# A fused attention, scan and spiking feed-forward kernel: rotary features by even and odd chunks, the bfloat16 split partly on GpSimd, and the norm of a tile moved up, in the projection stage

## The reference, cut to what matters

```python
ct_q = x @ Wd_q_w + Wd_q_b                       # x is normalised; 256 -> 128
query = heads(ct_q @ Wu_q_w + Wu_q_b) + heads(_rope(ct_q @ Wq_r_w + Wq_r_b, cos, sin))
ct_kv = x @ Wd_kv_w + Wd_kv_b
key = heads(ct_kv @ Wu_k_w + Wu_k_b) + heads(_rope(x @ Wk_r_w + Wk_r_b, cos, sin))
value = heads(ct_kv @ Wu_v_w + Wu_v_b)
# _rope: x0, x1 are the even and the odd features
out = jnp.stack([x0 * cos - x1 * sin, x1 * cos + x0 * sin], axis=-1)
```

## Time and profile before

| | us |
|---|---|
| three executions, median | 2242.89 |
| the profiled execution | 2247.14 |
| its span, first to last instruction | 2245.2 |
| mean granted TensorE clock | 0.944 |

### The profile page before, as it was taken

One profiled execution on the slowest core, in us unless ns is written; L12 is line 12 of the kernel. 1 busy time (PEld: TensorE's weight loads), 2 busy tenths in 40 slices (PEclk: granted clock), 3 DMA queues, 4 the chain that ended last, 5 costly groups with the idle time before them and its releaser, 6 DMA issues. The chain is left out here.

```text
span 2245.2 us, 26133 instructions
## 1 busy us (share of the span) xinstructions
PE 2016.3 (90%) x6926; PEld 747.5 (33%) x6926; DVE 1722.3 (77%) x2519; ACT 1117.6 (50%) x1448; POOL 673.0 (30%) x443
## 2 busy tenths in 40 slices
PE   6889799999999999999999988878878887679997
PEld 3444122233232332322444433333323332234443
DVE  4778889899898998974555556988898898935554
ACT  3444056666566666674233346566557556312221
POOL 0000200000000000000000017998898898910000
PEclk8999699999999999999999989999999998889998
DMA  3224322342222332204100013444444444310000
GB/s 106 78 81 102 58 34 44 51 55 44 40 44 39 55 51 40 44 16 132 52 0 0 0 40 94 112 108 107 109 106 110 112 108 109 96 39 10 19 19 28
DMA packets 99846, 139.76 MB, mean 62 GB/s; under 512 B 13408, under 2 KB 53104, under 8 KB 99728
## 3 DMA queue, kind: packets, MB, share of 16 engines
q1 hardware_dynamic: 99728, 138.30, 27.4%
HBM read 111.78 MB, written 26.08 MB: 61 GB/s over the span
## 5 line engine op out<-in xcount | busy, mean ns | idle before, releaser
L816 DVE TENSOR_REDUCE mx<-max_bank 128x1 f32<-128x512 f32 x960 | 618.3, 687 | 62.6 <-PE max_bank L714 62.2
L804 ACT ACTIVATE probs<-score_bank 128x1024 f32<-128x1024 f32 x512 | 496.9, 1021 | 298.0 <-PE score_bank L728 296.9
L1573 PE MATMUL ys_bank<-outs,rec_diag 128*128 128x512 f32 x512 | 281.3, 677 | 118.5 <-POOL outs L1509 106.6
L714 PE MATMUL max_bank<-ks,qs 96*128 96x512 bf16 x960 | 335.4, 390 | 0.0
L728 PE MATMUL score_bank<-qs,ks 99*128 99x512 bf16 x1024 | 313.5, 388 | 13.0 <-issue 11.8
L1501 POOL TENSOR_TENSOR ring<-u,bc 128x1024 f32<-128x1024 f32 x128 | 301.0, 2359 | 14.3 <-ACT u L1695 14.3
L1509 POOL TENSOR_TENSOR outs<-ring,bc 128x1024 f32<-128x1024 f32 x112 | 263.7, 2356 | 56.8 <-DVE ring L1908 56.8
L771 PE MATMUL o_bank<-probs,vg 128*32 128x512 f32 x2048 | 275.4, 610 | 0.5 <-ACT probs L804 0.5
L1746 ACT ACTIVATE a_bank<-dt,decay_s 128x512 f32<-128x512 f32 x256 | 171.2, 685 | 167.9 <-DVE ring L1908 153.5
L1249 PE MATMUL hid_bank_f<-xn_f,wfc_f 128*128 (+1 forms) x512 | 239.1, 600 | 8.3 <-DVE xn_f L997 5.1
L1327 DVE SCALAR_TENSOR_TENSOR hid_f<-hid_bank_f,relu_f 128x512 f32<-128x512 f32 x128 | 87.0, 690 | 199.0 <-ACT relu_f L1299 197.9
(11 more groups left out here) (200 smaller groups left out, 2145.2 us busy)
## 6 DMA issues: line engine op xcount, KB each, us to landing
bc<-bc_scr SPq DMA_DIRECT2D x128, 512.0 KB, 4.8
qk_parts<-parts SPq DMA_DIRECT2D x32, 384.0 KB, 2.9
ks<-qk_parts SPq DMA_DIRECT2D x96, 128.0 KB, 4.9
qs<-qk_parts SPq DMA_DIRECT2D x192, 64.0 KB, 5.1
o_scr<-o_sb SPq DMA_DIRECT2D x32, 256.0 KB, 2.0
xin<-in_x_dram SPq DMA_DIRECT2D x8, 512.0 KB, 4.2
o_in<-o_scr SPq DMA_DIRECT2D x16, 256.0 KB
out_dram<-x_out_f SPq DMA_DIRECT2D x8, 512.0 KB, 2.9
```

Of the source, the lines that this page charges most:

```text
L714: nc.tensor.matmul(max_bank[(r + a) % MB][:], qs[r][0:SROWS, half, j, qt * P:(qt + 1) * P], ks[r][0:SROWS, j, kh * TW:(kh + 1) * TW], star ...
L804: nc.scalar.activation(probs[:, s % 2, 2 * pair:2 * pair + 2], score_bank[pair][:], ACT.Exp, scale=SOFTMAX_SCALE).then_inc(probs_ready, 1)
L816: nc.vector.tensor_reduce(mx[:, a // HU, a % HU:a % HU + 1], max_bank[(r + a) % MB][:], AX_X, ALU.max)\
L1573: mm = nc.tensor.matmul(y_bank[f][:], rec_diag[:, f * NS + n], outs[:, g % OUTS, f], start=(n == 0), stop=(n == NS - 1))
```

## The change

Features of queries and keys are reordered: the weights' columns, biases and tables are laid out on the host so that chunk 0 holds the even feature of every pair and chunk 1 the odd one. A rotation then needs each rotary product once, and the swapped weights are not there any more. The scratch tensor in memory gets a layout with the partition rows of a stack in order, so a stack loads in 13 DMAs, and each of the four parts of a tile is written by four DMAs of 96 KB. The rests, the low parts and the scaling of x run on GpSimd. The sum with the compact product is written back into its bank. Banks: two for rotary products, two for compact ones, one for both latents, one for mean and variance, and the two for the transposes also hold the values. Transposes and mean run two tiles ahead, the variance one tile ahead. The table set with logarithm and exponential is requested once at the start. Loops over batches are written out.

```diff
-                 (wq[:, 0, :], io["Wu_q"]), (wq[:, 1, :], io["Wq_r"]), (wq[:, 2, :], io["Wq_r_swap"]),
-                 (wkr[:, 1], io["Wk_r_swap"].rearrange("(c p) n -> p c n", p=P)),
+        KV, ROT_K, Q, V, COMP_K, ROT_Q, COMP_Q = 0, 1, 3, 4, 6, 8, 10
+        UNITS = 12
...
         @block.sync
+            for t in range(NT):
+                if t + 3 < NT:
+                    load_x(t + 3)
+                if t == NT - TPB:
+                    for u in range(CHUNKS):
+                        sp.wait_ge(parts_out[u], OUT * t)
+                    load_stack(sp, split_scr, q_stack, k_stack, 0, stack_in)
                 for u in range(CHUNKS):
+                    sp.wait_ge(low_kept, t * CHUNKS + u + 1)
+                    side, c = 1 - u // DC, u % DC
+                    for n in range(NG):
+                        sp.dma_start(split_scr[(side * B + b) * NG + n, :, c * (HD // 2):(c + 1) * (HD // 2), :,
+                                               half * TW:(half + 1) * TW].rearrange("s i j t -> (i j) s t"),
+                                     parts[n * (P // NG):(n + 1) * (P // NG), u]).then_inc(parts_out[u], 16)
...
         @block.gpsimd
+            def lower_parts(t, side):
+                for u in (parts_of(side), parts_of(side) + 1):
+                    k = t * CHUNKS + u
+                    pool.wait_ge(high_kept, k + 1)
+                    if t:
+                        pool.wait_ge(low_kept, k - CHUNKS + 1)
+                    nc.gpsimd.tensor_tensor(rest[:, u], full[:, u], parts[:, u, 0], ALU.subtract).then_inc(rest_ready, 1)
+                for u in (parts_of(side), parts_of(side) + 1):
+                    pool.wait_ge(mid_kept, t * CHUNKS + u + 1)
+                    nc.gpsimd.tensor_tensor(parts[:, u, 2], rest[:, u], parts[:, u, 1], ALU.subtract).then_inc(low_kept, 1)
+            def scale(t):
+                pool.wait_ge(rs_step, t * 3 + 3)
+                if t > 1:
+                    pool.wait_ge(proj_ready, (t - 2) * UNITS + Q + 1)
+                for c in range(DC):
+                    nc.gpsimd.tensor_tensor(xn[:, t % 2, c], xc[:, c], rs[:], ALU.mult).then_inc(normed, 1)
+            scale(0)
+            for t in range(NT):
+                if t:
+                    lower_parts(t - 1, 0)
+                if t + 1 < NT:
+                    scale(t + 1)
+                lower_parts(t, 1)
+            lower_parts(NT - 1, 0)
...
         @block.tensor
+            def latent(t, u):
+                if u == 0:
+                    pe.wait_ge(latent_kept, t * 2 + 1)
+                elif t:
+                    pe.wait_ge(latent_kept, t * 2)
...
+            turn(0)
+            mean(0)
+            turn(1)
+            var(0)
+            mean(1)
+            pe.wait_ge(consts_in, CONSTS)
+            for t in range(NT):
                 pe.wait_ge(normed, t * DC + DC)
+                latent(t, 1)
+                rotary(t, 1)
+                latent(t, 0)
+                values(t)
+                compact(t, 1)
+                if t + 1 < NT:
+                    var(t + 1)
+                rotary(t, 0)
+                if t + 2 < NT:
+                    turn(t + 2)
+                compact(t, 0)
+                if t + 2 < NT:
+                    mean(t + 2)
...
         @block.scalar
+            nc.scalar.preload_act_table_set("natural_log_exp_and_others")
...
+            for t in range(NT):
+                if t:
+                    high(t - 1, 0)
+                keep_latent(t, 1)
+                keep_latent(t, 0)
+                if t + 1 < NT:
+                    square(t + 1)
+                if t:
+                    middle(t - 1, 0)
+                if t + 1 < NT:
+                    guess(t + 1)
+                if t + 2 < NT:
+                    keep_x(t + 2)
                 high(t, 1)
                 middle(t, 1)
+            high(NT - 1, 0)
+            middle(NT - 1, 0)
...
         @block.vector
+            def rotate(t, side):
+                for c, tables in enumerate(((cos, sin), (sin, cos))):
+                    dve.wait_ge(proj_ready, t * UNITS + (ROT_K if side == 1 else ROT_Q) + c + 1)
+                    for i, table in enumerate(tables):
+                        nc.vector.scalar_tensor_tensor(r[:, 2 * c + i], rot_bank[c][:], bias[:, c:c + 1], table,
+                                                       ALU.add, ALU.mult).then_inc(rotated, 1)
+            def join(t, side):
+                for c in range(DC):
+                    nc.vector.scalar_tensor_tensor(comp_bank[c][:], comp_bank[c][:], bias[:, c:c + 1], r[:, 3 * c],
+                                                   ALU.add, ALU.add).then_inc(rotated, 1)
+                for c in range(DC):
+                    nc.vector.tensor_tensor(full[:, u], comp_bank[c][:], r[:, 2 - c], ALU.subtract if c == 0 else ALU.add)\
+                        .then_inc(summed, 1)
...
+            for t in range(NT):
+                rotate(t, 1)
+                if t + 1 < NT:
+                    centre(t + 1)
+                keep_v(t)
+                join(t, 1)
+                if t + 1 < NT:
+                    finish(t + 1)
+                rotate(t, 0)
+                join(t, 0)
...
 def load_stack(eng, split_scr, q, k, g, done):
+    for row, part, n in K_RUNS:
+        eng.dma_start(k[row * HD:(row + n) * HD], k_in[part * HD:(part + n) * HD]).then_inc(done, 16)
+    for row, part, n in Q_RUNS:
         for h in range(2):
...
 def lay_out(v):
+    even = np.arange(D).reshape(NG, G, HD // 2, 2)[..., 0].transpose(0, 2, 1).reshape(P)
+    rows = np.concatenate([even, even + 1])
+        "cos": cos.T[even // 2], "sin": sin.T[even // 2],
...
-    qk_parts = nc.dram_tensor("qk_parts", (B * 2 * DC, P, 3, S), BF16, kind="Internal").ap()
+    qk_parts = nc.dram_tensor("qk_parts", (2 * B * NG, 3, HD, G, S), BF16, kind="Internal").ap()
```

More of the change, by code:

```diff
@@ L38, with runs_of @@
 MROWS = SROWS + 3
-STACK_LOAD = 16 * 3 * len(Q_PARTS)
+CHUNKS = 2 * DC
+def runs_of(parts):
+    found = []
+    for row, part in enumerate(parts):
+        if found and found[-1][1] + found[-1][2] == part:
+            found[-1][2] += 1
+        else:
+            found.append([row, part, 1])
+    return found
+Q_RUNS, K_RUNS = runs_of(Q_PARTS), runs_of(K_PARTS)
+STACK_LOAD = 16 * (len(K_RUNS) + 2 * len(Q_RUNS))
 LIF_STEPS, BETA, THRESHOLD = 5, 0.9, 1.0
@@ L104, in project @@
 def project(nc, io, xT, vT, split_scr, q_stack, k_stack):
-    CHUNKS = 2 * DC
+    SIDES = 2
     with ExitStack() as ctx:
@@ new lines, in compact, with values @@
+            def compact(t, side):
+                for c in range(DC):
+                    cols = slice(c * P, (c + 1) * P)
+                    if side == 0 or t:
+                        pe.wait_ge(summed, t * CHUNKS + (1 - side) * DC - DC + c + 1)
+                    mm = nc.tensor.matmul(comp_bank[c][:], wkc[:, cols] if side == 1 else wq[:, 0, cols], ct[:, side],
+                                          start=True, stop=True)
+                    mm.then_inc(proj_ready, 1)
+            def values(t):
+                pe.wait_ge(latent_kept, t * 2 + 1)
+                for pair in range(2):
+                    if t + 1 < NT:
+                        pe.wait_ge(x_kept, (t + 1) * DC + pair + 1)
+                    else:
+                        pe.wait_ge(v_kept, (t - 1) * 2 + pair + 1)
@@ new lines, in keep_latent, with high @@
+            def keep_latent(t, u):
+                act.wait_ge(proj_ready, t * UNITS + (Q if u == 0 else KV) + 1)
+                nc.scalar.activation(ct[:, u], lat_bank[:], ACT.Identity, bias=bcol[:, u:u + 1])\
+                    .then_inc(latent_kept, 1)
+            def high(t, side):
+                for u in (parts_of(side), parts_of(side) + 1):
+                    act.wait_ge(summed, t * CHUNKS + u + 1)
+                    act.wait_ge(parts_out[u], OUT * t)
+                    nc.scalar.activation(parts[:, u, 0], full[:, u], ACT.Copy).then_inc(high_kept, 1)
@@ L472, in _ @@
-            centre(0, 0)
-            finish(0, 0)
-            dve.wait_ge(consts_in, CONSTS)
-            tiles(dve, tile)
+            def rotate(t, side):
+                half = t % TPB
+                bias = bcol[:, 2 + 4 * side:4 + 4 * side]
+                cos, sin = (table[:, half * TW:(half + 1) * TW] for table in (cosT, sinT))
+                r = rot[:, 1 - side]
+                if t:
+                    dve.wait_ge(summed, (t - 1) * CHUNKS + parts_of(side) + DC)
+                for c, tables in enumerate(((cos, sin), (sin, cos))):
[3 more added lines that the diff above has]
+                                                       ALU.add, ALU.mult).then_inc(rotated, 1)
@@ L487, in load_stack @@
+    for row, part, n in Q_RUNS:
         for h in range(2):
-            eng.dma_start(q[rows, h], q_in[:, :, Q_PARTS[n], h * TW:(h + 1) * TW]).then_inc(done, 16)
+            eng.dma_start(q[row * HD:(row + n) * HD, h], q_in[part * HD:(part + n) * HD, :, h * TW:(h + 1) * TW])\
```

(1 more changed line is left out.)

353 lines of the change are left out of this document (119 added, 234 removed).

## The result

The changed kernel took 2172.0 us (median of 4 executions, 2169.9 to 2176.3) against 2245.4 us for the kernel before (4 executions, 2236.7 to 2249.3): 0.968 [0.965, 0.972]. It is faster, as forecast, but by more: 2185 us was the number and 2174 the lower end. Executed again with the later experiments it took 2173.1 us (6 executions, up to 2186.1) against 2242.4 (17 executions): 0.970 [0.967, 0.972].

What follows compares the result with a forecast made beforehand. Projection was taken as bound by TensorE's work plus waits from VectorE's queue. Stage: 22.2 + (18.8 + 2.6) + 6 x 18.8 + 30.3 = 186.7 us against 244.3, 57.6 less, so 2185 us; range 2174 to 2206.

Steps and rivals of the forecast that it cites:

- the norm chain: Projection, variance to scaled x: 6.5 us after the variance at 12.3, so 18.8 us against TensorE's own 18.4.
- Attention itself keeps its order: Attention stage: bounded by TensorE with its order kept, so no gain was counted.
- Start: Start of projection: first product moves from 23.0 to 22.2 us.
- The first tile's low clock: First projection tile: products at 1.2 GHz after TensorE waited, loss left at 2.6 us, bounds 0 and 2.6.
- A tile: Projection stage: 18.8 us a tile, against 27.35 before.
- The tail: Last tile's start to attention's first DMA: 30.3 us, where before it was 28.8, so 1.5 us longer.
- an attention of another length: Attention stage in the changed profile: a length other than before would show the prediction wrong; no size given.
- Both table loads in the norm chain: Rival, projection: two loads stay behind the variance, 2.57 us a tile, 18 in all, 2203 us; chance 0.04.
- The thinnest cover, 0.2 us before latent q: Projection tile: ScalarE's latent copy ends at 5.0 us, TensorE wants it at 5.2, 0.2 us of slack.
- Writing the join back into its bank: Projection, VectorE: writing the sum into its bank takes the same price, above by perhaps 0.1 us each.
- SyncE as the bound: Rival, projection: 16 small writes back up at 2.08 us an issue, 33.3 us a tile, 2299 us; chance 0.02.
- ScalarE's order binds: Rival, projection: slower GpSimd or hand-over delays latent q and variance, 20 to 21.5 us a tile, 2194 to 2204; chance 0.25.

Runs made afterwards that it cites:

- The tail experiment: Changed kernel with the last tile's four subtractions for q on VectorE and its last part written by four DMAs of ScalarE's queue: 2167.9 us.
- all on VectorE: Changed kernel with the eight subtractions and two scalings of a tile moved back from GpSimd to VectorE: 2190.6 us.
- the scaling on VectorE: Changed kernel with only the two scalings of x moved back from GpSimd to VectorE: 2184.1 us.
- the join from SBUF: Changed kernel with the sum of compact product and rotation written to SBUF, not back into its bank: 2175.4 us.

## Why the prediction came out as it did

The mechanism of a tile was right: TensorE's own work sets it, the norm chain adds a few tenths, GpSimd and SyncE hide. Two things put the number 13 us too high. Terms of the stage were sized too large, together 8.5 us; these alone would have left 2176.5 us, inside the range. The step that failed is the other one, "Attention itself keeps its order and is bounded by TensorE, so I give it nothing": with the same work the profiled executions show attention 4.8 us and the scan 6.1 us shorter.

The forecast stage was 186.7 us, the measured one 178.2 (179.8 when executed again). By its terms:

- **Start**, 22.2 forecast, 21.45 measured: 0.75 us.
- **The first tile's low clock**, 2.6 us added, none there in the profiled execution. The prediction named the bounds 0 and 2.6 and took the upper, from a start in which TensorE had stood still 6 us. After, it stands still only 2.41 and 1.88 us in this stretch, and ran at 2.4 GHz from 13.2 us on. In five of the six executions with this stage code the term was 0, in the sixth 2.1 us. The first tile took 18.46 us against 21.4, 2.9 us less with the tile's own difference.
- **A tile**, 18.8 forecast, 18.49 on the mean of six (39.91 to 150.87): 1.8 us. TensorE's part was exact: the variance product ends 12.30 us after the tile's start. From there to the next start it took 6.20 us, not 6.5: logarithm and exponential 1.35, Newton 2.15, scalings 2.50, and hand-overs 0.20 for which I had allowed 0.45.
- **The tail**, 30.3 forecast, 27.3 measured: 3.0 us. VectorE's last sum ended 17.7 us after the tile's start, not 18.5; from there the last lower part took 4.6 us, not 5.3, since subtractions with a bfloat16 operand or result take GpSimd 1.155 us, not 1.27, and ScalarE's copies overlap them; the last issue then started 2.2 us later, at 24.5 us, not 2.5, with an issue at 0.44 us, not 0.54; and from the last issue to attention's first it took 2.8 us, not 4.0. In the execution again the tail was 29.0 us, for the low clock of its last tile, which the prediction had not foreseen either.

These make 8.5 us. What lies outside the stage is 10.9 us by the two profiles; the profiled execution before was 4.2 us above the median that the forecast used, the one after 2.0 us below its own, so by the medians 4.5 us are left of the 13. Between the measured medians it is 3 to 9 us (73.4 and 69.3 us less in all, less 66.1 or 64.5). In attention it is the time that TensorE's clock stays at the lower level behind its short waits, 21.5 us against 35.4; in the scan it is whether the clock is low over its first 8 us. What places an execution in one or the other wasn't found: not the number of loads, and a start delayed by 2 to 7 us moved attention by under 2 us and the scan not at all. The tail experiment had a scan of 635.5 and the best median, so one profiled execution doesn't even tell what a kernel does as a rule, and whether the change has any lasting part in it stays open. The prediction's range had allowed 5 us for the differences between executions, and nothing for stages behind that run shorter with the same code, though its last paragraph names an attention of another length as a sign of being wrong. (That range has a slip at its upper end as well: 2204 and 5 us are 2209, not 2206.)

The other statements of the prediction:

- *Both table loads in the norm chain* (the "loads stay" rival, 18 us): one of the two. Its price was 13.5 to 15.1 us in the stage, by another way: 1.28 us a tile, and the rest in a late start and a low clock in the first and the last tile.
- *The thinnest cover, 0.2 us before latent q*: the copy ended at 44.37 us, the product started at 45.17, so 0.8 us. The copy came 0.54 us earlier than laid out; about half of that is GpSimd's shorter subtractions, the rest ScalarE's high parts, two in 1.13 us and not 1.3. Its place was right: latent q is where TensorE waits in three experiments (all on VectorE 2.17, the scaling on VectorE 0.97, the join from SBUF 0.17 us).
- *Writing the join back into its bank*: 680 ns for the last sum, no dearer, as I had taken it.
- *SyncE as the bound*: 16 issues at 0.44 us are 7.0 us a tile. No sign of it.
- *ScalarE's order binds* (0.25): not at these durations. An operation of 1.6 us on GpSimd, which it needed, appeared only where the two engines collide.

## What to carry to other kernels

A wait is worth what ends last there: one request for a table set gave 2.4 us of the stage in the old order and 13.5 to 15.1 in the new one, and in both the loads were equally plain to see. Before a short operation is moved to the faster engine, see what runs on GpSimd at that moment: two SBUF inputs on VectorE beside a GpSimd read can cost more than the engine's speed gives back. And when one stage is changed, compare that stage in the traces, since here unchanged stages differ by up to 10 us from one kernel to the next.

## What the hardware showed that I had not expected

- VectorE and GpSimd taking turns costs both: VectorE's sum has a mean of 1.24 us in place of 0.68, GpSimd's subtraction 1.40 in place of 1.16.
- GpSimd's 128x512 operation takes 1.27 us with float32 throughout, 1.155 us where one operand or the result is bfloat16 (the first are a product and a sum, the second subtractions; a subtraction in float32 throughout wasn't measured). The two small tiles of the earlier trace rows (0.42 and 0.42 us) had suggested no difference.
- A table load can stand ahead of the wait of its activation (2.4 us before the logarithm in the experiment without the request) or behind it. Ahead of it, a load of 1.28 us can cost nothing.
- TensorE's clock fell to 1.2 GHz after some waits of 2.4 to 2.9 us and not after others of like length. The same code ran with the clock low at its first product in one execution (3.75 us for four instructions) and full in another (1.95 us).
- The clock over the first 8 us of a stage of 630 us went with 6 us of its length (a clock of 0.50 to 0.54 in the five long scans, 1.00 in the nine short ones).
